# Moving the first layer norm's normalisation and the unrouted rows to ScalarE in an attention and mixture-of-experts kernel

## The reference, cut to what matters

```
x  = layernorm(x + attention(x))            # x: 4 batches, 2048 tokens, 256 features
     # Q, K = sign(x * sign(b)), V = x * sign(bv); scores = Q K^T / 16, causal
     # attention = sigmoid(4 * scores) V, zero above the diagonal
x  = layernorm(x + moe(x))
     # router: logits = x @ w_router (32 experts), softmax, the best expert, its probability as gate
     # each expert takes at most 320 tokens, in order; the others get nothing added
     # expert: (silu(x Wg) * (x Wu)) Wd, times the gate
```

## Time and profile before

| | |
|---|---|
| median of 3 runs | 687.56 us (684.07 to 689.95) |
| span of the profiled execution | 678.2 us, first to last instruction |
| attention stage within it | about 16 to 380 us |
| tail | about 380 to 410 us |
| experts' stage | about 410 to 678 us |

### The profile page before, as it was taken

One profiled execution on the slowest core, in us unless ns is written; L12 is line 12 of the kernel. 1 busy time (PEld: TensorE's weight loads), 2 busy tenths in 40 slices (PEclk: granted clock), 3 DMA queues, 4 the chain that ended last, 5 costly groups with the idle time before them and its releaser, 6 DMA issues.

```text
span 678.2 us, 14737 instructions
## 1 busy us (share of the span) xinstructions
PE 604.2 (89%) x4175; PEld 504.3 (74%) x4214; DVE 485.0 (72%) x1300; ACT 353.4 (52%) x678; POOL 415.3 (61%) x547
## 2 busy tenths in 40 slices
PE   5989898899879898988999879999999999999960
PEld 4878787698768687876888637877788778878750
DVE  2669978879787989698898624666776677766740
ACT  5566566456455655666555312555445554555520
POOL 4563757467857377765576520566666666676773
PEclk9999999999999899899999998999999999999995
DMA  8962021132201112206111020566555565566300
GB/s 273 368 211 78 32 80 59 37 96 94 94 29 62 50 39 93 86 23 219 58 59 49 31 87 28 148 193 187 169 158 176 171 190 168 159 184 195 118 32 21
DMA packets 68206, 78.11 MB, mean 115 GB/s; under 512 B 7934, under 2 KB 59374, under 8 KB 68160
## 3 DMA queue, kind: packets, MB, share of 16 engines
q1 hardware_dynamic: 60992, 63.26, 30.1%
q0 software_dynamic: 7168, 14.30, 5.9%
HBM read 44.29 MB, written 37.90 MB: 121 GB/s over the span
## 4 chain that ended last, share of the span: by engine, by line
PE 68%; DVE 9%; issue 8%; ACT 6%; POOL 5%; DMA 2%; SPq 0%; ACTq 0%; DVEq 0%; POOLq 0%
PE ps L877 13%; PE ps L738 8%; PE ps L739 6%; PE ps L740 6%; PE ps L862 6%; PE ps L864 5%; PE ps L863 5%; PE ps L716 5%; PE ps L846 5%; PE ps L765 4%; DVE hl_ring L929 4%; DVE xrow L957 2%; PE ps L757 2%; ACT hl_ring L574 2%; POOL out_dram L490 2%
## 5 line engine op out<-in xcount | busy, mean ns | idle before, releaser
L738 PE MATMUL ps<-v_hl,hl_ring 128*128 128x256 f32 x544 | 176.6, 325 | 25.6 <-DVE hl_ring L929 16.7
L739 PE MATMUL ps<-v_hl,hl_ring 128*128 128x256 f32 x544 | 156.0, 287 | 0.0
L740 PE MATMUL ps<-v_hl,hl_ring 128*128 128x256 f32 x544 | 155.6, 286 | 0.0
L738 PEld LDWEIGHTS ps<-v_hl,hl_ring 128*128 128x128 f32 x544 | 105.9, 195 | 51.5 <-issue 28.4
L490 POOL DMA_INDIRECT out_dram<-alone,ids x96 | 108.0, 1125 | 55.8 <-ACT alone L665 22.5
L572 ACT ACTIVATE a_ring<-ps 128x512 f32<-128x512 f32 (+3 forms) x160 | 85.7, 535 | 91.1 <-PE ps L716 49.9
L929 DVE TENSOR_TENSOR hl_ring<-a_ring,hl_ring 128x512 fp32r<-128x512 f32 (+3 forms) x160 | 119.1, 748 | 19.0 <-ACT hl_ring L574 8.8
L409 POOL DMA_INDIRECT expert_rows<-xrow,slot x64 | 68.7, 1074 | 63.9 <-issue 26.1
L739 PEld LDWEIGHTS ps<-v_hl,hl_ring 128*128 128x128 f32 x544 | 106.2, 195 | 1.9
L740 PEld LDWEIGHTS ps<-v_hl,hl_ring 128*128 128x128 f32 x544 | 106.0, 195 | 0.0
L877 PE MATMUL ps<-xall,a_ring 128*128 128x256 f32 (+1 forms) x384 | 95.9, 392 | 1.1 <-DVE a_ring L1107 1.1
(11 more groups left out here) (108 smaller groups left out, 1125.3 us busy)
## 6 DMA issues: line engine op xcount, KB each, us to landing
expert_rows<-xs SPq DMA_DIRECT2D x40, 258.0 KB, 5.6
xs<-expert_rows SPq DMA_DIRECT2D x32, 258.0 KB, 3.0
xall<-in_L_attn_x_dram SPq DMA_DIRECT2D x16, 512.0 KB, 4.1
out_dram<-alone SPq DMA_DIRECT2D x16, 512.0 KB, 3.1
xall<-in_L_ffn_w_gate_dram SPq DMA_DIRECT2D x32, 256.0 KB, 3.6
xall<-in_L_ffn_w_up_dram SPq DMA_DIRECT2D x32, 256.0 KB, 3.9
xall<-in_L_ffn_w_down_dram SPq DMA_DIRECT2D x32, 256.0 KB, 4.2
xs<-expert_rows SPq DMA_DIRECT2D x32, 64.5 KB, 3.0
```

Of the source, the lines that this page charges most:

```text
L738: mm(o, ah, v_hl[:, 0, j, :], start=(j == 0), stop=False)
L739: mm(o, ah, v_hl[:, 1, j, :], start=False, stop=False)
L740: last = mm(o, al, v_hl[:, 0, j, :], start=False, stop=(j == GT * g + i))
```

## The change

The normalisation leaves VectorE and becomes four ScalarE activations (Identity, with the factor as scale and minus mean times factor as bias), one a tile. The alone rows leave GpSimd and become four ScalarE activations (Copy, with the factor as scale). `rstd` gets two more small operations, for minus the mean and its product with the factor; `small` is doubled so that two groups can be under way. The statements for the token numbers stay on GpSimd under the name `rows_numbered`, and now wait for the earlier scatter of the same buffer. VectorE's `residual` has a new wait for the normalisation two groups back. NORM becomes a step for each tile, and ALONE is new.

```diff
-NORM = {3: (3, 4), 0: (13, 13), 1: (21, 21), 2: (29, 29)}
+NORM = {3: (3, 3, 4, 4), 0: (10, 11, 12, 13), 1: (18, 19, 20, 21), 2: (28, 28, 29, 29)}
+ALONE = {3: (7, 8, 10, 10), 0: (16, 17, 18, 19), 1: (24, 25, 26, 27), 2: (32, 34, 36, 38)}
...
             def store_alone(G, par):
-                atleast(sp, alone_ready, G + 1)
+                atleast(sp, alone_ready, (G + 1) * GT)
...
-                atleast(pool, alone_ready, G, settle=True)
+                atleast(pool, alone_ready, (G - 1) * GT, settle=True)
...
+                g_.tensor_scalar(small[:, par, 0, :], var, EPS, None, ALU.add).then_inc(rstd_step, 1)
+                g_.tensor_tensor(small[:, par, 6, :], mv[:, :, 0], mone[:, :], ALU.mult).then_inc(rstd_step, 1)
                 atleast(pool, rstd_step, base + 2, settle=True)
+                g_.tensor_tensor(small[:, par, 1, :], small[:, par, 0, :], mhalf[:, :], ALU.pow).then_inc(rstd_step, 1)
                 atleast(pool, rstd_step, base + 3, settle=True)
+                g_.tensor_tensor(small[:, par, 7, :], small[:, par, 6, :], small[:, par, 1, :], ALU.mult).then_inc(rstd_step, 1)
...
-                g_.tensor_tensor(alone[:, par, :, :], xrow[:, par, :, 0:D],
-                                 small[:, 5, :].unsqueeze(2).broadcast_to([P, GT, D]), ALU.mult)\
-                    .then_inc(alone_ready, 1)
+            def rows_numbered(G, half, par):
+                atleast(pool, scattered[par], half * 16 * GT, settle=True)
...
+            def normalise(G, turn, par, tiles=range(GT)):
+                act.wait_ge(rstd_step, G * RN + 4)
+                atleast(act, scattered[par], turn * 16 * GT)
+                for i in tiles:
+                    s_.activation(xrow[:, par, i, 0:D], res[par][:, i, :], ACT.Identity,
+                                  bias=small[:, par, 7, i:i + 1], scale=small[:, par, 1, i:i + 1]).then_inc(x1_ready, 1)
+
+            def rows_alone(G, half, par, tiles=range(GT)):
+                act.wait_ge(rstd_step, (G + 1) * RN)
+                act.wait_ge(x1_ready, (G + 1) * GT)
+                atleast(act, alone_out[par], half * 16)
+                for i in tiles:
+                    s_.activation(alone[:, par, i, :], xrow[:, par, i, 0:D], ACT.Copy,
+                                  scale=small[:, par, 5, i:i + 1]).then_inc(alone_ready, 1)
...
             copy_x1t(B * NG - 1)
             gates(B * NG - 1)
+            rows_alone(B * NG - 1, 2 * B - 1, 1)
...
             def residual(G, i, done, par):
                 dve.wait_ge(pv_done, done)
+                atleast(dve, x1_ready, (G - 1) * GT)
...
-            def normalise(G, turn, par, tiles=range(GT)):
-                dve.wait_ge(rstd_step, G * 6 + 2)
-                dve.wait_ge(mv_ready, (G + 1) * GT)
-                atleast(dve, scattered[par], turn * 16 * GT)
-                for i in tiles:
-                    v_.tensor_scalar(xrow[:, par, i, 0:D], res[par][:, i, :], mv[:, i, 0:1], small[:, 1, i:i + 1],
-                                     ALU.subtract, ALU.mult).then_inc(x1_ready, 1)
```

More of the change, by code:

```diff
@@ L495, in _ @@
             rstd(last + 3, 1)
-            rows_alone(last + 3, 2 * B - 1, 1)
+            rows_numbered(last + 3, 2 * B - 1, 1)
             scatter(last + 3, 1)
@@ L605, in batch @@
                         bb = b - 1 if g == 3 else b
+                        turn = 2 * b + {3: -1, 0: 0, 1: 0, 2: 1}[g]
+                        for i in range(GT):
+                            if k == NORM[g][i]:
+                                normalise(bb * NG + g, turn, g % 2, range(i, i + 1))
                         if k == COPY[g]:
@@ L609, in batch @@
                             gates(bb * NG + g)
+                        for i in range(GT):
+                            if k == ALONE[g][i]:
+                                rows_alone(bb * NG + g, turn, g % 2, range(i, i + 1))
                     if first and k == 3:
@@ L1049, in batch @@
                         G = (b - 1 if g == 3 else b) * NG + g
-                        turn = 2 * b + {3: -1, 0: 0, 1: 0, 2: 1}[g]
                         if k == STATS[g]:
                             statistics(G, g % 2)
-                        for half in range(2):
-                            if k == NORM[g][half]:
-                                normalise(G, turn, g % 2, range(half * GT // 2, (half + 1) * GT // 2))
                         if k in (PICK[g], PICK[g] + 1):
@@ L1081, in _ @@
             low_weights(0, 0)
-            normalise(G, 2 * B - 1, 1)
             low_weights(0, 1)
```

33 lines of the change are left out of this document (14 added, 19 removed).

## The result

| | before | after |
|---|---|---|
| median of 4 runs each, same chip | 688.75 us (684.07 to 693.30) | 714.74 us (710.72 to 720.06) |
| ratio after / before | | 1.0385, 95% interval 1.0315 to 1.0456 |
| span of the profiled execution | 678.2 us | 714.2 us |
| mean granted clock of TensorE | 0.965 | 0.938 |

The account below looks back on a forecast made before the run. TensorE was taken to set the pace, VectorE next. The terms 6.6 + 4.5 + 8.1 - 5.6 + 1.0 made +14.6 us, rounded to +14: 701.5 us, with a range of 683 to 713.

Parts of the forecast that it names:

- 9.4 us around it that stays: Profiled span lies 9.4 us below the median of the runs, taken as time around it that stays.
- Steps 3 and 4: Group 3, three batches: ScalarE held for GpSimd's factor, sigmoids 3.8 us late, TensorE +2.2 by step 7; +6.6 us.
- 10 to 12: Three batches: three tiles ahead of the values' high half delay GpSimd's L364 and the low half it blocks; +4.5 us.
- 18 to 24: Three batches: ScalarE waits for group 1's factor behind group 3's scatter, step 19 starts 3.9 us late; +8.1 us.
- Steps 28 to 32: Forecast as steps 28 to 30, four batches: short stall, step 29 delayed 0.9 us, xrow waits and slow stretches go; -5.6 us.
- relief rival: Steps 3 and 18: factor there in time or stall swallowed, so the gain of 16 us remains, 671.5 us; chance 0.11.
- stores on SP: Alone rows' stores move a few steps later, x loads behind them needed at least five steps on; costed at nothing.
- alone tiles: Steps 16, 17, 24 to 27, 32 to 38: tiles stand where ScalarE idles for TensorE; nothing, 24 us at worst.
- the clock falls more often: Rival: the new TensorE waits bring six more slow stretches at 1.0 us each, +6 us, 707.5 us; chance 0.10.
- half-swallowed stalls: Rival: waits on VectorE behind the stalls shrink and absorb part of them, +0 to +7 us, about 690; chance 0.22.
- the signs named: ScalarE idle 3 to 4 us at steps 3 and 18; batches 2 to 4 longer by 3 to 6; VectorE down 43 or more.
- The tail: After the last step: four tiles on ScalarE end at 386.7, TensorE's transposes at about 387.0 instead of 386.02; +1.0 us.

Follow-up runs that it names:

- the repeats: The changed kernel run again without further edits on two other chips: 715.97 and 716.85 us, ratios 1.0527 and 1.0529 to the kernel before.
- The late placement: Changed kernel with normalised tiles moved later: group 3 all at step 4, group 1 at 20, 20, 21, 21, group 2 all at 29; 698.45 us, ratio 1.0259.
- the last series: Changed kernel, normalised tiles at TensorE's steps, alone tiles early, plus: step 10 free of tiles 0.9993; few idle matmuls 1.0007; both 0.9944.
- the run with the early alone tiles: Changed kernel with group 2's alone tiles after steps 31 to 34 instead of 32, 34, 36 and 38: 713.51 us, ratio 1.0482.
- The half with the alone rows alone: Changed kernel with the normalisation back on VectorE: 689.02 us, ratio 1.0132; with early alone tiles and few idle matmuls added, 684.56 us, 1.0054.
- the fill: Changed kernel with idle matmuls into an unused PSUM bank at TensorE's waits (steps 4, 11, 12, 19, 29): 704.41 us, ratio 1.0354.
- the control: Kernel before with idle matmuls at its own longer waits (4 at steps 11 and 12, 6 at step 29): 679.31 us, ratio 0.9976.

## Why the prediction was right or wrong

**The base.** "9.4 us around it that stays" was wrong: it is 1.8 us. The profiled execution of before had simply been quicker than all three shown. This put 7.6 us on the forecast, and it hid that the change was sized far too small: 14.6 us for 36.0.

**Steps 3 and 4, 10 to 12, 18 to 24.** Right in mechanism and near in sum: 6.6, 4.5, 8.1 us forecast, 7.0, 3.9 and 9.0 found, the first 9.4 and 9.5 in the repeats. The stall of ScalarE was forecast with 3.8 us at step 3 and came with 3.4, 1.2 and 3.2; at step 18 it was forecast with 3.9 and came with 2.7, 2.7 and 2.5. That the sum of steps 18 to 24 came out all the same was in part luck. The late placement (ratio 1.0259) shows that the tiles' place is the cause, and the last series shows their price at step 10, 0.3 us each rather than the 0.5 taken. By batch the first is not even: 4.1, 0.4 and 1.8 us for steps 0 to 10. In the third batch the gap at the jump had already made TensorE late by 3.5 us, and the stall fell into it: without the gap the same steps lose 4.2 us.

**Steps 28 to 32: the step that failed.** -5.6 us forecast, +4.1 found, 9.7 of the 21 us missing. The forecast was 0.9 us of delay for step 29 in each of four batches, "so the stall is short", and 9.2 us of gains behind it. Step 29 came 2.7, 3.2, 3.1 and 2.7 us late, 11.7 instead of 3.6, and that is 8.1 of the 9.7; the gains behind it were 7.6. The rows of the third batch that show it:

```profile
286.53 1.09 ACT L584 ACTIVATE xrow<-res,small 128x256 f32<-128x256 f32 x2 [2.02 <-POOL small L383]
288.45 2.35 POOL L366 TENSOR_TENSOR v_hl<-z,v_hl 128x1024 fp32r<-128x1024 f32 x1
289.62 1.73 DVE L951 TENSOR_TENSOR hl_ring<-a_ring,hl_ring 128x512 fp32r<-128x512 f32 x1 [2.15 <-ACT hl_ring L570]
291.06 2.52 POOL L359 TENSOR_TENSOR z<-xall,bv_row 128x1024 f32<-128x1024 f32 x1 [0.25 <-POOL v_hl L366]
291.57 2.57 DVE L951 TENSOR_TENSOR hl_ring<-a_ring,hl_ring 128x512 fp32r<-128x512 f32 x1 [0.21 <-ACT hl_ring L570]
291.50 0.56 PE L760 MATMUL ps<-v_hl,hl_ring 128*128 128x256 f32 x1 [1.31 <-ACT hl_ring L570]
```

Two things add up. ScalarE stands 2.02 us for the factor (1.7 to 2.0 in all four batches) and then does two tiles, so step 29's sigmoids start 2.8 us late (4.57 us after the ones ahead of them, where they started 1.73 us after them in the kernel before). And being late, the low halves of steps 29 and 30 fall beside GpSimd's products of the values and take 1.73 and 2.57 us where 0.68 is the free length. In the kernel before it was VectorE's normalisation that stood there, for 5.48 us in all where four tiles take 1.38 alone:

```profile
265.76 5.48 DVE L957 TENSOR_SCALAR xrow<-res,mv,small 128x256 f32<-128x256 f32 x4
```

The forecast read the blocked normalisation as a burden to be thrown off and did not ask who would stand beside the products next. Two runs part the two causes. With the products moved away, step 29 is still 2.0 to 2.1 us late in three batches: that is the stall and the tiles. With the tiles at step 29 and the products where they were, step 29 is not late at all, its low half takes 0.69 us, and the gains are 8.9 us, close to the 9.2 forecast. So the gains were right; the delay ahead of them was not, and the block was a consequence of the delay, not of the normalisation's leaving alone.

The Trainium skill (SBUF — State Buffer, section "Who interferes with whom") has a VectorE instruction with two SBUF inputs and a GpSimd instruction that reads SBUF exclude each other, and ScalarE free of both; the trace agrees, with the rows above and with ScalarE's two tiles at 289.43 us, beside L366, that took 1.08 us together. Drawn on for the relief rival, that rule says what becomes of the moved operation; it does not say which one meets the lock next.

**Nothing for the stores on SP.** They were costed at nothing, with loads "needed at least five steps on". Nobody waits for their data, and still 3.5 us were lost at the jump, which the run with the early alone tiles did not lose there (0.2 us). Why the next instructions were late stays open.

**Nothing for the alone tiles.** The cover named for them, ScalarE's idling for TensorE, holds: at steps 16 to 18 nothing is lost, and the 0.9 us of batches 2 and 3 at steps 24 to 28 are 0.1 or less in both repeats. The half with the alone rows alone loses 1.3% even so; its trace has 3.2 us at the jump, and 2.6 us at steps 10 to 12 and 4.1 at steps 12 to 18, behind the two tiles of step 10. 0.5% are left when the gap and the clock are mended.

**The clock.** The rival "the clock falls more often" had the right mechanism, at 6 us and a chance of 0.10. It was not a rival but a term that the stalls bring with them: 12.4 us by the fill, about 9 of them the change's own by the control, where I had put nothing into the sum. The stretches can be seen in the windows of after: 0.50 behind step 12 in all four batches (42 to 44, 140 to 144, 246 to 250 and 348 to 352 us), where before had them in batches 2 and 3 only. In steps 12 to 18 the forecast has nothing, and 3.8 us were lost.

**The rivals and the signs.** Relief did not come: the two steps' lead of the scores hides no stall of 3 us. The half-swallowed stalls are in the trace once, in batch 3. Of the signs named, ScalarE's idle stretches came three times each at steps 3 and 18, but only two of the six were 3 to 4 us long. TensorE did stop waiting for xrow at step 29. Batch 1 was longer by 0.9 us, and batches 2 to 4 by 9.8 (with the jump's 3.5 left out), 6.1 and 12.2 us, not by 3 to 6. VectorE's busy time fell by 41.6 us, not 43 or more, as the low halves took over blocked time, 126.1 us for all where it was 119.1. A tile cost 0.49 to 0.50 us (2.08 for four in the tail), as taken. The tail cost 2.3 us up to the end of the transposes, not 1.0. The first tile starts 1.4 us later after the last step than VectorE's did, where 0.4 had been taken: two operations more in GpSimd's chain, one of them 1.13 us long (L379). The transposes come in pairs behind the tiles, 0.5 us apart on ScalarE where VectorE's came 0.33 apart, 2.08 us for 1.32; the clock, 0.64 in this stretch and 1.00 before, has a smaller part in it:

```profile
419.55 2.08 ACT L584 ACTIVATE xrow<-xs,small 128x256 f32<-128x256 f32 x4 [7.07 <-POOL small L383]
420.30 2.08 PE L779 MATMUL ps<-ident,xrow 128*128 128x128 f32 x8 [3.27 <-ACT xrow L584]
```

## What to carry to other kernels

When work is moved to an engine that feeds the bound one in written order, place it after the moment at which its input is there, even if the engine idles earlier: the same 128 tiles cost 36 us in one table of steps and nothing that the runs could tell in another. When an operation that was blocked by a neighbour is taken away, look up which operation will now stand beside that neighbour, at the time at which it will really start, and who waits for it. And price every new wait of TensorE twice, once for its length and once for the slow clock behind it.

## What the runs showed of the hardware that was not expected

- A change of less than 1 us in when VectorE's low half starts decided between 0.56 us and 2.58 us for it, by whether it came before or after the start of GpSimd's 2.4 us product.
- At the loop's jump VectorE stood 3.9 to 5.6 us without a visible cause, instead of 2.4 to 2.9 us for ScalarE, when a store and a load (235 GB/s in the window) were released just before it. With the store a few steps earlier the gap was gone, and at the starts of batches 2 and 4, where no loop jumps back, the same transfers cost nothing. Its cause is open.
- Idle matmuls gave back 12.4 us of the changed kernel's time and 1 us of the kernel before's. Where TensorE had no wait to fill, they cost 1.3 and 2.1 us a batch at each place and ate what the clock gave.
